# A cross-attention pair: VectorE transposes x of the first batch of every second pair from blocks

## The chip, the core and the metric

The kernel runs on one core of a Trainium2 chip. The metric is the device time of one execution in microseconds. The kernel before took 321.79, 327.54 and 326.51 us in three runs, median 326.51; the execution that was profiled took 321.73 us.

## The reference

Inputs are x and ctx (called y in the kernel), each 32 batches of 128 channels by 1024 positions, float32, and small weight matrices of 128 x 128. Two layers follow one another:

- Layer 0, twice a channel attention with 8 heads of 16 channels: queries from x, keys and values from y, and the other way round. The scores are sums over all 1024 positions, so each head has a 16 x 16 matrix; softmax over its rows; values times attention, and a projection. The two results are added to x + y.
- Layer 1: queries and keys from y (with biases), values from the output of layer 0, again channel attention with 8 heads, an output projection, a residual, and a normalisation over all 128 x 1024 elements of a batch with a gain and shift per channel.

```
attn = softmax(einsum('bhni,bhnj->bhij', q, k) * scale)      # layer 0, both directions
scores = einsum('bhdl,bhel->bhde', q, k) / sqrt(E)            # layer 1
o = Wo @ (attn @ v) + bo + x;  o_hat = (o - mean) * rsqrt(var + eps) * gn_w + gn_b
```

## The kernel before

Since all scores are sums over positions, the kernel never forms queries or keys. For each batch it computes one Gram matrix of (y, 1, x) over positions (gram_chunks), 128 x 257, and gets the scores of all three attentions from it with weight products (u12_products, u3_products, scores). The attention matrices are folded with the weights into one matrix per input (z_products, m_products, pq_products), P for x and Q for y, and the output is P x + Q y + shift (out_half), with each operand split into a high part and a low rest. pq_high (ScalarE) and pq_low (VectorE) split P and Q; split_high (ScalarE) and split_low (GpSimd) split x and y. Then come the moments and the normalisation.

Work goes in steps step(h, u), one for each pair of batches p = 2h + u; the four batches of an h are n = 4h + 2u + b with a buffer (slot) 2u + b each. A step does the Gram matrices of pair p, the scores and attention of pair p - 1, and the output of pair p - 2. Steps 2 to 15 take the branch `front` with `back` set; of these, u = 1 holds for h = 1 to 7. From h = 2 the steps lie in a hardware loop with two steps in a pass.

A Gram matrix needs positions on the partitions, so x and y must be transposed into the tile t (positions x (y, 1, x)). This is done in two ways. TensorE transposes x of the first batch of a pair (b = 0) from the natural layout (x_transpose of the PE block, L345), four 128 x 128 pieces a call into the PSUM tile tpx, and ScalarE copies each half into t (xt_out, L637). VectorE transposes y of both batches and x of the second from y_blocks and x_blocks (y_transpose L867, x_transpose L877), tiles that the DMA has already loaded with the blocks rearranged so that 32 x 32 transposes finish the job. A half batch is one such instruction.

Every engine runs its list in the written order, and semaphores order the engines: xt_ready and yt_ready (halves transposed), n_ready (n3_out on VectorE done, L1020), pq_done, pqhi_ready, pqlo_ready, u3_ready, attn_ready. Two PSUM banks called mid0 and mid1 are used in turn: u12_products, then the scores in mid0; pq_products, then u3_products in mid1. pq_low reads mid1 after pq_high has; so u3_products waits for pqlo_ready of its own step. u12_products waits for c_ready (c_out), and z_operands, before the last chunk of the pair's Gram matrices, for attn_ready.

The SP queue loads what comes next in its own order: for each step refill_blocks of the first batch, refill_raw of a batch of the pair before, refill_blocks of the second batch (with load_x_blocks), refill_raw of the first batch. Each waits until the buffer is free.

In the order of TensorE before the change, the front of each step is

```
x_transpose(h, u, 0)
pq_products(p - 2)
x_transpose(h, u, 1)
u12_products(p - 1)
out_half(h - 1, u, 0, 0)
u3_products(p - 1)
```

Of the kernel before, what the change touches and what calls it, by code (L numbers as in the profile page):

```python
# [6 lines left out]
B, C, N, H = 32, 128, 1024, 8  # L7
# [3 lines left out]
HC = CH // 2  # L11
HALF = N // 2
QUADS = 4
# [14 lines left out]
def cross_attention_pair_kernel(nc, x, y, weights, vectors, quad_rows, consts, out):  # L28
# [13 lines left out]
    with ctx:  # L42
        def sb(name, shape, dt=f32):
            return ctx.enter_context(nc.sbuf_tensor(name, shape, dt))
# [4 lines left out]
        def sem(name):  # L49
            return ctx.enter_context(nc.semaphore(name))  # L50
# [23 lines left out]
        mask6 = sb("mask6", [C, 6, W32])  # L74
        raw = [sb(f"raw{n}", [C, 2, N]) for n in range(4)]
        y_blocks = [sb(f"y_blocks{n}", [C, QUADS, N // QUADS]) for n in range(4)]
        x_blocks = [sb(f"x_blocks{n}", [C, QUADS, N // QUADS]) for n in range(2)]
        xy_hi = [sb(f"xy_hi{n}", [C, 2, N], f32r) for n in range(4)]
        xy_lo = [sb(f"xy_lo{n}", [C, 2, N], f32r) for n in range(4)]

# [54 lines left out]
        x_in = [sem(f"x_in{n}") for n in range(4)]  # L135
        y_in = [sem(f"y_in{n}") for n in range(4)]
        blocks_in = [sem(f"blocks_in{n}") for n in range(4)]
        x_blocks_in = [sem(f"x_blocks_in{n}") for n in range(2)]
        x_half_in = [sem(f"x_half_in{n}") for n in range(2)]
        y_half_in = [sem(f"y_half_in{n}") for n in range(2)]  # L140
        stored = [sem(f"stored{n}") for n in range(4)]
# [70 lines left out]
        def before(h, u):  # L212

            return (h - 1, 0) if u == 1 else (h - 2, 1)
# [7 lines left out]
        @block.sync  # L222
        def _(sp):
            def load_x(h, n):
                sp.dma_start(raw[n][:, 0, :], x[4 * h + n]).then_inc(x_in[n], 16)

            def load_y(h, n):
                sp.dma_start(raw[n][:, 1, :], y[4 * h + n]).then_inc(y_in[n], 16)

            def load_blocks(h, n):  # L230

                blocks = y[4 * h + n].rearrange("(i c) (a m) -> a c i m", c=W32, a=QUADS)
                for a in QUAD_ORDER:
                    sp.dma_start(y_blocks[n][W32 * a:W32 * (a + 1), :, :], blocks[a]).then_inc(blocks_in[n], 16)

            def load_x_blocks(h, u):

                blocks = x[4 * h + 2 * u + 1].rearrange("(i c) (a m) -> a c i m", c=W32, a=QUADS)
                for a in QUAD_ORDER:
                    sp.dma_start(x_blocks[u][W32 * a:W32 * (a + 1), :, :], blocks[a]).then_inc(x_blocks_in[u], 16)  # L240

            sp.dma_start(cst[:, :], consts).then_inc(consts_in, 16)
            for i in range(2):
                cols = slice(HALF * i, HALF * (i + 1))
                sp.dma_start(raw[0][:, 0, cols], x[0][:, cols]).then_inc(x_half_in[i], 16)
                sp.dma_start(raw[0][:, 1, cols], y[0][:, cols]).then_inc(y_half_in[i], 16)
            load_x(0, 1)
            load_y(0, 1)
            sp.dma_start(vec[:, :], vectors).then_inc(weights_in, 16)
            sp.dma_start(quad[:, :, :], quad_rows).then_inc(weights_in, 16)  # L250
            sp.dma_start(wt[:, :, :], weights).then_inc(weights_in, 16)
            k = WNAMES.index("prT")
            sp.dma_start(w_rot[0:H64, :, :], weights[H64:C, k:k + 2, :]).then_inc(weights_in, 16)
            sp.dma_start(w_rot[H64:C, :, :], weights[0:H64, k:k + 2, :]).then_inc(weights_in, 16)
            for n in range(2, 4):
                load_x(0, n)
                load_y(0, n)
            load_blocks(1, 0)
            load_blocks(1, 1)
            load_x_blocks(1, 0)  # L260

            def raw_free(h, u, b):

                n = 4 * h + 2 * u + b
                sp.wait_ge(split_hi, 2 * n + 2)
                sp.wait_ge(split_lo, 2 * n + 2)
                if isinstance(n, int) and n < 4:
                    sp.wait_ge(y_early_done, 2 * n + 2)
                    sp.wait_ge(x_transposed[b], n - b + 2)
                elif b == 0:  # L270
                    sp.wait_ge(x_transposed[0], n + 2)

            def refill_raw(h, u, b):
                raw_free(h, u, b)
                load_x(h + 1, 2 * u + b)
                load_y(h + 1, 2 * u + b)

            def refill_blocks(h, u, b):
                n = 4 * h + 2 * u + b
                sp.wait_ge(yt_ready, 2 * n + 2)  # L280
                load_blocks(h + 1, 2 * u + b)
                if b == 1:
                    sp.wait_ge(xt_ready[1], n + 1)
                    load_x_blocks(h + 1, u)

            def store(h, u, b):
                q = 4 * h + 2 * u + b - 4
                sp.wait_ge(normed, q + 3)
                if q == B - 1:
                    sp.wait_ge(last_normed, 1)  # L290
                sp.dma_start(out[q], res[2 * u + b][:, :]).then_inc(stored[2 * u + b], 16)

            def step(h, u):
                refill_blocks(h, u, 0)
                refill_raw(h - 1 + u, 1 - u, 1)
                refill_blocks(h, u, 1)
                refill_raw(h, u, 0)

            refill_raw(0, 0, 0)
            load_blocks(1, 2)  # L300
            refill_raw(0, 0, 1)
            load_blocks(1, 3)
            load_x_blocks(1, 1)
            refill_raw(0, 1, 0)
            with sp.Fori(1, PAIRS // 2 - 1) as i:
                step(i, 0)
                step(i, 1)
            last = PAIRS // 2 - 1
            refill_raw(last - 1, 1, 1)
            store(last + 1, 0, 0)  # L310
            store(last + 1, 0, 1)
            store(last + 1, 1, 0)
            store(last + 1, 1, 1)
            for n in range(4):
                sp.wait_ge(stored[n], 16 * (B // 4 + 1))
# [3 lines left out]
        def _(pe):  # L319
# [15 lines left out]
            def x_transpose(h, u, i):  # L335

                p = 2 * h + u
                if i == 0:
                    pe.wait_ge(x_in[2 * u], 16 * (h + 1))
                if isinstance(p, int) and p == 2:  # L340
                    pe.wait_ge(xt_ready[1], 3 + i)
                pe.wait_ge(xt_ready[0], 2 * p - 1 + i)
                chunks = raw[2 * u][:, 0, :].rearrange("c (r m) -> c m r", m=CH)
                for c in range(HC):
                    mm = pe.transpose(tpx[i][:, c, :], chunks[:, HC * i + c], ident)  # L345
                mm.then_inc(x_transposed[0], 1)
# [188 lines left out]
            def step(h, u, front, middle, back, post):  # L535
# [32 lines left out]
                    gram_full_width(h, u, 1, 5, 8)  # L568
                    m_products(p - 1, False)
                elif front:  # L570
                    x_transpose(h, u, 0)
                    pq_products(p - 2)
                    x_transpose(h, u, 1)
                    u12_products(p - 1)
                    out_half(h - 1, u, 0, 0)
                    u3_products(p - 1)
                    if post:
                        group_moments(p - 3)
                    out_half(h - 1, u, 0, 1)
# [49 lines left out]
        def _(act):  # L629
            def xt_out(h, u, b, i):  # L630

                slot = 2 * u + b
                n = 4 * h + slot
                act.wait_ge(x_transposed[b], 2 * (2 * h + u) + i + 1)
                if i == 0 and not (isinstance(n, int) and n < TB):
                    act.wait_ge(gram_done, n - TB + 1)
                act.activation(t[slot][:, HC * i:HC * (i + 1), XC:GW], tpx[i][:, :, :], ACT.Copy)\  # L637
                    .then_inc(xt_ready[b], 1)
# [95 lines left out]
            def step(h, u, front, middle, back, post):  # L734
# [23 lines left out]
                    z_out(p - 1)  # L758
                    gram_out(p, 1)
                elif front:  # L760
                    xt_out(h, u, 0, 0)
                    pq_high(p - 2, u)
                    xt_out(h, u, 0, 1)
                    u12_out(p - 1)
                    split_high(h - 1 + u, 1 - u, 1, 0, post)
                    keys_times_sums(p - 1)
# [49 lines left out]
        def _(dve):  # L816
# [49 lines left out]
                dst = t[slot][:, HC * i:HC * (i + 1), 0:C].rearrange("p m (i c) -> p m i c", c=W32)  # L866
                dve.transpose(dst, blocks[:, HC * i:HC * (i + 1)]).then_inc(yt_ready, 1)  # L867

            def x_transpose(h, u, i):

                n = 4 * h + 2 * u + 1
                if i == 0:
                    dve.wait_ge(x_blocks_in[u], 16 * QUADS * h)
                    dve.wait_ge(gram_done, n - TB + 1)
                blocks = x_blocks[u][:, :, :].rearrange("p i (c m) -> p m i c", c=W32)
                dst = t[2 * u + 1][:, HC * i:HC * (i + 1), XC:GW].rearrange("p m (i c) -> p m i c", c=W32)
                dve.transpose(dst, blocks[:, HC * i:HC * (i + 1)]).then_inc(xt_ready[1], 1)  # L877

            def gram_mirror(p):

# [148 lines left out]
            def step(h, u, front, middle, back, post, ahead=True):  # L1029
# [7 lines left out]
                elif front and not back:  # L1037
# [10 lines left out]
                    n3_out(p - 1)  # L1048
                    c_out(p - 1, 1 - u)
                    gram_mirror(p)  # L1050
                elif front:
                    if post:
                        half_stats(*before(h, u), 1, 1)
                        half_moments(p - 3)
# [4 lines left out]
                    u3_out(p - 1)  # L1059
                    if post:  # L1060
                        variance(p - 3, 1 - u)
                    x_transpose(h, u, 0)
                    shift_scores(p - 1)
                    x_transpose(h, u, 1)
                    softmax_out(p - 1)
                    half_stats(h - 1, u, 0, 0)
                    half_stats(h - 1, u, 0, 1)
                    if ahead:
                        y_transpose(h + u, 1 - u, 0, 0)
                        y_transpose(h + u, 1 - u, 0, 1)  # L1070
                    gram_mirror(p)
                    half_stats(h - 1, u, 1, 0)
                    n12_out(p - 1)
# [131 lines left out]
```

## Time and profile before

| | before |
|---|---|
| median of 3 runs | 326.51 us (321.79 to 327.54) |
| profiled execution | 321.73 us |
| its span | 319.9 us |
| TensorE matmul busy | 307.0 us, 96% |
| TensorE weight load busy | 269.3 us, 84% |
| VectorE busy | 262.2 us, 82% |
| ScalarE busy | 233.0 us, 73% |
| GpSimd busy | 190.0 us, 59% |
| DMA | 73.87 MB, mean 231 GB/s |
| mean granted TensorE clock | 0.994 |

The span is the time from the first to the last instruction of the profiled execution; the device time includes what lies around it. Busy times are unions of the instructions' spans; matmuls overlap, so their mean duration is longer than the step from one to the next. The chain of waits, followed back from the last instruction, gives pieces without overlap.

### The profile page before, as it was taken

To read this page: it belongs to the slowest core of one execution; us is meant where nothing else is said; L and a number is where in the kernel's file an instruction comes from. 1 tells how busy PE (TensorE), PEld (TensorE's weight loads), DVE (VectorE), ACT (ScalarE), POOL (GpSimd) and SP (SyncE) were. 2 spreads that over 40 slices of the span, in tenths; PEclk is the share of its full clock that TensorE was granted. 3 is DMA by queue.
4 is the path that set the end of the run, shared out by engine and by line. 5 is a ranking of instruction groups with operands and counts; after the bars stand their busy time and mean duration, and the time that the engine had idled before them with its cause. 6 is when DMAs were issued, how large, how long until landed. Compare 5 with 4: busy or idle time off the path is not lost.

```text
span 319.9 us, 12574 instructions
## 1 busy us (share of the span) xinstructions
PE 307.0 (96%) x4792; PEld 269.3 (84%) x4792; DVE 262.2 (82%) x707; ACT 233.0 (73%) x385; POOL 190.0 (59%) x277
## 2 busy tenths in 40 slices
PE   7999999999998999999999999999999999999980
PEld 4887898988888798888989888898988889898760
DVE  2495897889998688988888899988888898976883
ACT  3654656878778577887878787797878779786485
POOL 0866291767656376664647676464667656465620
PEclk9999999999999999999999999999999999999997
DMA  7999969499896949979696978969696976130036
GB/s 223 386 276 321 280 189 274 120 299 232 270 308 185 310 141 309 256 226 324 181 317 192 304 228 275 310 168 332 190 291 204 304 220 207 56 131 0 2 131 262
DMA packets 39060, 73.87 MB, mean 231 GB/s; under 512 B 4608, under 2 KB 26368, under 8 KB 39040
## 3 DMA queue, kind: packets, MB, share of 16 engines
q1 hardware_dynamic: 35008, 58.92, 64.1%
q10 hardware_dynamic: 4032, 14.68, 13.2%
q8 instruction: 13, 0.21, 0.3%
q14 instruction: 7, 0.06, 0.1%
HBM read 56.81 MB, written 16.78 MB: 230 GB/s over the span
## 4 chain that ended last, share of the span: by engine, by line
PE 92%; DVE 2%; issue 2%; DMA 2%; ACT 1%; SPq 1%; POOLq 0%; POOL 0%
PE oacc L428 10%; PE oacc L435 9%; PE oacc L429 8%; PE mid L531 5%; PE gacc L388 4%; PE mid L455 4%; PE mid L508 4%; PE stat L390 4%; PE tpx L345 4%; PE gacc L389 3%; PE stat L388 3%; PE gacc L390 3%; PE stat L389 3%; PE mid L517 2%; PE gacc L406 2%; PE mid L518 2%
## 5 line engine op out<-in xcount | busy, mean ns | idle before, releaser
L1136 POOL TENSOR_TENSOR xy_lo<-raw,xy_hi 128x256 fp32r<-128x256 f32 x256 | 179.4, 739 | 113.5 <-ACT xy_hi L705 113.5
L705 ACT ACTIVATE xy_hi<-raw 128x1024 fp32r<-128x1024 f32 x64 | 67.0, 1049 | 0.0
L867 DVE STREAM_TRANSPOSE t<-y_blocks 128x512 f32<-128x512 f32 x56 | 62.4, 1154 | 0.0
L712 ACT ACTIVATE res<-oacc 128x512 f32<-128x512 f32 x59 | 34.9, 593 | 27.9 <-PE oacc L435 27.6
L428 PE MATMUL oacc<-xy_hi,pq_hi 128*128 128x512 f32 x120 | 52.3, 436 | 0.1
L896 DVE BATCH_NORM_STATS2 hstat<-res 128x6 f32<-128x512 f32 x60 | 40.1, 687 | 14.0 <-ACT res L712 14.0
L429 PE MATMUL oacc<-xy_lo,pq_hi 128*128 128x512 f32 x120 | 47.3, 394 | 0.5 <-issue 0.5
L391 PE MATMUL gacc<-t 128*32 128x225 f32 x224 | 45.3, 354 | 0.0
L390 PE MATMUL gacc<-t 128*32 128x225 f32 x224 | 45.3, 354 | 0.0
L391 PE MATMUL stat<-t 128*32 128x225 f32 x224 | 44.9, 353 | 0.0
L390 PE MATMUL stat<-t 128*32 128x225 f32 x224 | 44.9, 353 | 0.0
L389 PE MATMUL gacc<-t 128*32 128x161 f32 x224 | 44.3, 300 | 0.0
L389 PE MATMUL stat<-t 128*32 128x161 f32 x224 | 43.9, 299 | 0.0
L388 PE MATMUL stat<-t 128*32 128x129 f32 x224 | 43.0, 272 | 0.8 <-issue 0.8
L388 PE MATMUL gacc<-t 128*32 128x129 f32 x224 | 42.9, 273 | 0.0
L726 ACT ACTIVATE res<-res,nbias,nscale 128x1024 f32<-128x1024 f32 x30 | 37.2, 1242 | 5.2 <-issue 4.3
L435 PE MATMUL oacc<-xy_hi,pq_lo 128*128 128x512 f32 x120 | 38.6, 404 | 0.0
L392 PE MATMUL gacc<-t 128*32 128x96 f32 x224 | 36.8, 246 | 0.0
L392 PE MATMUL stat<-t 128*32 128x96 f32 x224 | 36.8, 246 | 0.0
L877 DVE STREAM_TRANSPOSE t<-x_blocks 128x512 f32<-128x512 f32 x28 | 31.9, 1139 | 0.0
L393 PE MATMUL gacc<-t 128*32 128x64 f32 x224 | 30.8, 219 | 0.0
L393 PE MATMUL stat<-t 128*32 128x64 f32 x224 | 30.7, 219 | 0.0
(166 smaller groups left out, 906.1 us busy)
## 6 DMA issues: line engine op xcount, KB each, us to landing
raw<-in_x SPq DMA_DIRECT2D x31, 512.0 KB, 5.2
raw<-in_ctx SPq DMA_DIRECT2D x31, 512.0 KB, 6.4
y_blocks<-in_ctx SPq DMA_DIRECT2D x112, 128.0 KB, 6.5
out<-res ACTq DMA_DIRECT2D x28, 512.0 KB, 3.4
x_blocks<-in_x SPq DMA_DIRECT2D x56, 128.0 KB, 6.3
out<-res SPq DMA_DIRECT2D x4, 512.0 KB, 2.7
wt<-in_weights SPq DMA_DIRECT2D x1, 896.0 KB, 7.0
raw<-in_x SPq DMA_DIRECT2D x2, 256.0 KB, 3.5
```

What stands on the lines that cost most here:

```text
L388: pe.matmul(acc[0:W32, C:GW], wa, tb[:, c, C:GW], start=first, stop=False)
L389: pe.matmul(acc[3 * W32:C, 3 * W32:GW], wd, tb[:, c, 3 * W32:GW], start=first, stop=False)
L390: pe.matmul(acc[W32:H64, W32:GW], wb, tb[:, c, W32:GW], start=first, stop=final)
L391: pe.matmul(acc[H64:3 * W32, W32:GW], wc, tb[:, c, W32:GW], start=first, stop=final)
L392: pe.matmul(acc[0:W32, 0:3 * W32], wa, tb[:, c, 0:3 * W32], start=False, stop=final)
L393: mm = pe.matmul(acc[3 * W32:C, 0:H64], wd, tb[:, c, 0:H64], start=False, stop=final)
L428: pe.matmul(bank[:, :], whi, xy_hi[slot][:, s, cols], start=(s == 0), stop=False)
L429: pe.matmul(bank[:, :], whi, xy_lo[slot][:, s, cols], start=False, stop=False)
L435: mm = pe.matmul(bank[:, :], pq_lo[u][:, b, s, :], xy_hi[slot][:, s, cols], start=False, stop=(s == 1))
L705: act.activation(xy_hi[slot][:, s, :], raw[slot][:, s, :], ACT.Copy).then_inc(split_hi, 1)
L867: dve.transpose(dst, blocks[:, HC * i:HC * (i + 1)]).then_inc(yt_ready, 1)
L1136: piece = pool.tensor_tensor(xy_lo[slot][:, s, cols], raw[slot][:, s, cols], xy_hi[slot][:, s, cols].bitcast(f32), ALU.subtract)
```

## The change

VectorE now also transposes x of the first batch (b = 0) of the pairs with u = 1, from a third x_blocks tile, so slots 1, 2 and 3 have one. TensorE's x_transpose and ScalarE's xt_out remain for u = 0 only. In the u = 1 steps u3_products moves in front of the first output half. On VectorE, the first half of that transpose stands at the end of the u = 0 step, and the u = 1 step has an order of its own: pq_low directly behind half_stats, then the moments, the second half of the transpose, and y_transpose in two separate calls around u3_out and variance. The SP queue loads the third tile (four DMAs of 128 KB) in the u = 1 step behind refill_raw, after a wait on xt_ready[0], and once at the start.

```diff
-        x_blocks = [sb(f"x_blocks{n}", [C, QUADS, N // QUADS]) for n in range(2)]
+        x_blocks = {n: sb(f"x_blocks{n}", [C, QUADS, N // QUADS]) for n in (1, 2, 3)}
...
 # SP
-                elif b == 0:
-                    sp.wait_ge(x_transposed[0], n + 2)
+                elif b == 0 and u == 0:
+                    sp.wait_ge(x_transposed[0], 2 * h + 4)
...
             def step(h, u):
                 refill_blocks(h, u, 0)
                 refill_raw(h - 1 + u, 1 - u, 1)
+                if u == 1:
+                    sp.wait_ge(xt_ready[0], 4 * h + 4)
+                    load_x_blocks(h + 1, 2)
                 refill_blocks(h, u, 1)
                 refill_raw(h, u, 0)
...
             refill_raw(0, 0, 1)
+            load_x_blocks(1, 2)
             load_blocks(1, 3)
-            load_x_blocks(1, 1)
+            load_x_blocks(1, 3)
...
 # TensorE
                 elif front:
-                    x_transpose(h, u, 0)
+                    if u == 0:
+                        x_transpose(h, u, 0)
                     pq_products(p - 2)
-                    x_transpose(h, u, 1)
+                    if u == 0:
+                        x_transpose(h, u, 1)
                     u12_products(p - 1)
+                    if u == 1:
+                        u3_products(p - 1)
                     out_half(h - 1, u, 0, 0)
-                    u3_products(p - 1)
+                    if u == 0:
+                        u3_products(p - 1)
...
 # ScalarE
-                    xt_out(h, u, 0, 0)
+                    if u == 0:
+                        xt_out(h, u, 0, 0)
                     pq_high(p - 2, u)
-                    xt_out(h, u, 0, 1)
+                    if u == 0:
+                        xt_out(h, u, 0, 1)
...
 # VectorE: x_transpose takes a batch b
-            def x_transpose(h, u, i):
+            def x_transpose(h, u, b, i):
+                slot = 2 * u + b
+                n = 4 * h + slot
                 if i == 0:
-                    dve.wait_ge(x_blocks_in[u], 16 * QUADS * h)
+                    dve.wait_ge(x_blocks_in[slot], 16 * QUADS * h)
                     dve.wait_ge(gram_done, n - TB + 1)
...
+                dve.transpose(dst, blocks[:, HC * i:HC * (i + 1)]).then_inc(xt_ready[b], 1)
...
 # VectorE, u = 0: as before, and at its end
+                    c_out(p - 1, 1 - u)
+                    x_transpose(h, 1, 0, 0)
 # VectorE, u = 1
+                elif front:
+                    half_stats(*before(h, u), 1, 1)
+                    pq_low(p - 2, u)
+                    half_moments(p - 3)
+                    partition_moments(p - 3, 1 - u)
+                    x_transpose(h, u, 0, 1)
+                    y_transpose(h, u, 1, 0)
+                    u3_out(p - 1)
+                    variance(p - 3, 1 - u)
+                    y_transpose(h, u, 1, 1)
+                    x_transpose(h, u, 1, 0)
+                    shift_scores(p - 1)
+                    x_transpose(h, u, 1, 1)
                     softmax_out(p - 1)
                     half_stats(h - 1, u, 0, 0)
                     half_stats(h - 1, u, 0, 1)
```

## Rows read from the trace of the kernel before

**Rows 1.** The page: busy us, share of the span, instructions of each engine.

```profile
PE 307.0 (96%) x4792; PEld 269.3 (84%) x4792; DVE 262.2 (82%) x707; ACT 233.0 (73%) x385; POOL 190.0 (59%) x277
```

**Rows 2.** Busy by window, one whole step: PE, PEld, DVE, ACT, POOL, clock, DMA, GB/s.

```profile
163.30:181.70 18.40, 18.37 (x319) 16.45 (x318) 16.25 (x43) 14.44 (x24) 11.94 (x18) 1.00 0.86 253
```

**Rows 3.** The chain of waits at the head of pair 9's step: start us, us, what.

```profile
163.33 0.44 PE tpx L345 x4
163.77 0.89 PE mid L531 x8
164.66 0.44 PE tpx L345 x4
165.10 0.87 PE mid L455 x4
165.97 0.23 PE oacc L428
...
167.35 0.44 PE mid L464 x4
167.80 0.12 PE stat L442 x2
...
169.41 0.25 PE mid L475 x8
```

**Rows 4.** Groups of instructions, TensorE's transposes: count, busy us, mean ns, idle before.

```profile
L345 PE MATMUL tpx<-cst,raw 128*128 128x128 f32 x112 | 16.9, 274 | 0.0
```

**Rows 5.** Timelines, pairs 0 and 2: start us, us, engine, line, idle before it.

```profile
20.01 0.71 PE L464 MATMUL mid<-wt,gram 128*128 128x128 f32 x4
...
33.27 0.43 DVE L1020 TENSOR_TENSOR nmat<-mid,cst 128x256 f32<-128x256 f32 x1
33.75 1.16 PE L531 MATMUL mid<-nmat 128*128 128x128 f32 x8
34.95 0.60 ACT L684 ACTIVATE pq_hi<-mid 128x512 fp32r<-128x512 f32 x1 [0.62 <-PE mid L531]
35.58 0.69 DVE L889 TENSOR_TENSOR pq_lo<-mid,pq_hi 128x512 fp32r<-128x512 f32 x1 [0.73 <-ACT pq_hi L684]
```

**Rows 6.** Timeline of VectorE from the end of pair 8's step through pair 9's.

```profile
162.86 0.42 DVE L1020 TENSOR_TENSOR nmat<-mid,cst 128x256 f32<-128x256 f32 x1
163.20 0.21 DVE L1026 TENSOR_SCALAR cshift<-mid,vec 128x2 f32<-128x2 f32 x1
163.99 0.70 DVE L896 BATCH_NORM_STATS2 hstat<-res 128x6 f32<-128x512 f32 x1 [0.58 <-ACT res L712]
...
165.50 0.68 DVE L889 TENSOR_TENSOR pq_lo<-mid,pq_hi 128x512 fp32r<-128x512 f32 x1
166.10 2.22 DVE L867 STREAM_TRANSPOSE t<-y_blocks 128x512 f32<-128x512 f32 x2
168.25 0.56 DVE L970 SCALAR_TENSOR_TENSOR u<-wt,gram,mid 128x128 f32<-128x128 f32 x2
...
173.74 0.36 DVE L990 TENSOR_REDUCE ssum<-mid 128x6 f32<-128x192 f32 x1 [0.95 <-ACT mid L668]
...
174.66 0.56 DVE L1005 TENSOR_TENSOR attn<-mid,sinv 128x384 f32<-128x384 f32 x1
...
179.87 0.70 DVE L896 BATCH_NORM_STATS2 hstat<-res 128x6 f32<-128x512 f32 x1 [0.29 <-ACT res L712]
```

**Rows 7.** The chain of waits, first Gram chunk and the end of the last.

```profile
170.04 0.27 PE gacc L388
...
176.40 0.60 PE mid L508 x16
```

**Rows 8.** Timelines of GpSimd and of the SP queue in pair 9's step.

```profile
170.40 0.70 POOL L1143 TENSOR_TENSOR rstd<-var,cst 128x2 f32<-128x2 f32 x1
...
174.00 0.35 SPq L225 DMA_DIRECT2D raw<-in_x  x1
...
178.01 2.53 SPq L240 DMA_DIRECT2D x_blocks<-in_x  x4
```

**Rows 9.** Busy by window, a stretch with idle TensorE; and the longest transpose.

```profile
28.00:32.00 4.00, 3.76 (x37) 2.64 (x36) 0.70 (x1) 2.10 (x4) 2.78 (x4) 1.00 1.07 322
...
L867 DVE STREAM_TRANSPOSE t<-y_blocks x56: 1060/1144/1237, 26.6 to 277.4; 128x512 f32<-128x512 f32 x56
```

More of the change, by code:

```diff
@@ L137, in cross_attention_pair_kernel @@
         blocks_in = [sem(f"blocks_in{n}") for n in range(4)]
-        x_blocks_in = [sem(f"x_blocks_in{n}") for n in range(2)]
+        x_blocks_in = {n: sem(f"x_blocks_in{n}") for n in (1, 2, 3)}
         x_half_in = [sem(f"x_half_in{n}") for n in range(2)]
@@ L234, in load_blocks, with load_x_blocks @@
                     sp.dma_start(y_blocks[n][W32 * a:W32 * (a + 1), :, :], blocks[a]).then_inc(blocks_in[n], 16)
-            def load_x_blocks(h, u):
-                blocks = x[4 * h + 2 * u + 1].rearrange("(i c) (a m) -> a c i m", c=W32, a=QUADS)
+            def load_x_blocks(h, n):
+                blocks = x[4 * h + n].rearrange("(i c) (a m) -> a c i m", c=W32, a=QUADS)
                 for a in QUAD_ORDER:
-                    sp.dma_start(x_blocks[u][W32 * a:W32 * (a + 1), :, :], blocks[a]).then_inc(x_blocks_in[u], 16)
+                    sp.dma_start(x_blocks[n][W32 * a:W32 * (a + 1), :, :], blocks[a]).then_inc(x_blocks_in[n], 16)
             sp.dma_start(cst[:, :], consts).then_inc(consts_in, 16)
@@ L259, in _ @@
             load_blocks(1, 1)
-            load_x_blocks(1, 0)
+            load_x_blocks(1, 1)
             def raw_free(h, u, b):
@@ L283, in refill_blocks @@
                     sp.wait_ge(xt_ready[1], n + 1)
-                    load_x_blocks(h + 1, u)
+                    load_x_blocks(h + 1, 2 * u + 1)
             def store(h, u, b):
@@ L633, in xt_out @@
                 n = 4 * h + slot
-                act.wait_ge(x_transposed[b], 2 * (2 * h + u) + i + 1)
+                if isinstance(n, int) and n < 4:
+                    act.wait_ge(x_transposed[b], 2 * u + i + 1)
+                else:
+                    act.wait_ge(x_transposed[0], 2 * h + 3 + i)
                 if i == 0 and not (isinstance(n, int) and n < TB):
@@ L867, in y_transpose @@
                 dve.transpose(dst, blocks[:, HC * i:HC * (i + 1)]).then_inc(yt_ready, 1)
-            def x_transpose(h, u, i):
-                n = 4 * h + 2 * u + 1
+            def x_transpose(h, u, b, i):
+                slot = 2 * u + b
+                n = 4 * h + slot
                 if i == 0:
-                    dve.wait_ge(x_blocks_in[u], 16 * QUADS * h)
+                    dve.wait_ge(x_blocks_in[slot], 16 * QUADS * h)
                     dve.wait_ge(gram_done, n - TB + 1)
-                blocks = x_blocks[u][:, :, :].rearrange("p i (c m) -> p m i c", c=W32)
-                dst = t[2 * u + 1][:, HC * i:HC * (i + 1), XC:GW].rearrange("p m (i c) -> p m i c", c=W32)
-                dve.transpose(dst, blocks[:, HC * i:HC * (i + 1)]).then_inc(xt_ready[1], 1)
+                blocks = x_blocks[slot][:, :, :].rearrange("p i (c m) -> p m i c", c=W32)
+                dst = t[slot][:, HC * i:HC * (i + 1), XC:GW].rearrange("p m (i c) -> p m i c", c=W32)
+                dve.transpose(dst, blocks[:, HC * i:HC * (i + 1)]).then_inc(xt_ready[b], 1)
             def gram_mirror(p):
@@ L1050, in step @@
                     gram_mirror(p)
-                elif front:
+                elif front and u == 0:
                     if post:
@@ L1061, in step @@
                         variance(p - 3, 1 - u)
-                    x_transpose(h, u, 0)
+                    x_transpose(h, u, 1, 0)
                     shift_scores(p - 1)
-                    x_transpose(h, u, 1)
+                    x_transpose(h, u, 1, 1)
+                    softmax_out(p - 1)
+                    half_stats(h - 1, u, 0, 0)
+                    half_stats(h - 1, u, 0, 1)
+                    y_transpose(h, 1, 0, 0)
+                    y_transpose(h, 1, 0, 1)
+                    gram_mirror(p)
+                    half_stats(h - 1, u, 1, 0)
+                    n12_out(p - 1)
+                    n3_out(p - 1)
+                    c_out(p - 1, 1 - u)
[10 more added lines that the diff above has]
+                    y_transpose(h, u, 1, 1)
+                    x_transpose(h, u, 1, 0)
+                    shift_scores(p - 1)
+                    x_transpose(h, u, 1, 1)
                     softmax_out(p - 1)
@@ L1068, in step @@
                     if ahead:
-                        y_transpose(h + u, 1 - u, 0, 0)
-                        y_transpose(h + u, 1 - u, 0, 1)
+                        y_transpose(h + 1, 0, 0, 0)
+                        y_transpose(h + 1, 0, 0, 1)
                     gram_mirror(p)
```

## The prediction

> **What bounds the kernel now.** I read the busy table first, then one step in the steady part, then its chain of waits, then the timelines of the two engines that the change touches. The table puts TensorE at 96% of the span and VectorE at 82% [rows 1]. In one whole step of the later part, a u = 1 step (pair 9), TensorE is busy for 18.37 of 18.40 us at full clock, VectorE for 16.25 [rows 2]. The steady step is therefore the sum of TensorE's own work, and anything TensorE need not do is worth its full length, provided that nothing makes it wait in its place. The busy time alone does not settle the price, since matmuls overlap; the chain gives the step from one piece to the next, and I take all prices from it.
>
> In that chain the head of the step has no idle piece [rows 3]: first group of four transposes 0.44 us, pq_products 0.89, second group of transposes 0.44 (164.66 to 165.10), u12_products 0.87, first half of the output 1.38 (165.97 to 167.35), u3_products 0.44 (0.45 by the starts), group_moments and the second half 1.61 (167.80 to 169.41), then scores. From 163.33 to 169.41 that is 6.08 us.
>
> **What is removed.** The reordered branch is the one for u = 1, h = 1 to 7: 7 steps. Each loses 8 TensorE transposes, 2 x 0.44 = 0.88 us, 6.2 us in all. As a check, the 112 transposes of the whole run are busy for 16.9 us [rows 4], which gives 8.4 for 56 by the busy time; that counts overlapped tails, so 6.2 stands and 8.4 is the far end of the gain. Two ScalarE copies per step go too; ScalarE waits elsewhere in the step and they are worth nothing by themselves.
>
> **What the transposes were hiding, at pq_products.** It waits for n3_out on VectorE, which ends at 162.86 + 0.42 = 163.28 [rows 6]. Before, four transposes ran in front of it. Now it is first. Pair 2's step shows a start straight after that wait: n3_out ends at 33.27 + 0.43 = 33.70, the matmuls begin at 33.75 and take 1.16 us to the end instead of the 0.89 of a running stream [rows 5]. So: start at 163.33, end at 164.49 rather than 163.33 + 0.89 = 164.22. Cost 0.27 us.
>
> **The wait that appears, at u3_products.** It writes the bank mid1, and its wait on pqlo_ready is met only by this step's pq_low, which reads the same bank. Where it stood, behind the first output half, that was past. Now only u12_products stands between. The path is pq_products, pq_high on ScalarE, pq_low on VectorE, then u3_products. Pair 2 shows its length: the products end at 33.75 + 1.16 = 34.91, pq_high starts at 34.95, and pq_low ends at 35.58 + 0.69 = 36.27 [rows 5], 1.36 us. From 164.49 this gives 165.85, and with 0.05 more to wake TensorE, 165.90. u12_products ends at 164.49 + 0.87 = 165.36. A restarted u3_products takes 0.71 us (pair 0, [rows 5]), so it ends at 166.61 instead of 165.80. Cost 0.81 us.
>
> VectorE could be later than that: in front of pq_low stands now x_transpose(h, 1, 0, 0), moved to the end of the u = 0 step, and half_stats. c_out starts at 163.20 with 0.21; one transpose steps on 1.08 (2.15 for two, 166.10 to 168.25) and half_stats 0.65 to 0.70 [rows 6]. 163.35 + 1.08 + 0.68 = 165.11, against pq_high's end at 164.49 + 0.04 + 0.60 = 165.13. The transpose fits into the 0.58 us that VectorE waited before half_stats, plus what the pq path leaves; nothing is added, but the margin is nil.
>
> **The sum.** Per step -0.88 + 0.27 + 0.81 = +0.20 us; scores would start at 169.61. Seven steps: +1.4 us. As lower end I let both restarts cost nothing beyond the idle time between slots: 0.16 (163.33 against the free slot, which lies one overlapped tail of about 0.16 before the end at 163.33) and 0.70, so -0.02 per step, or -0.1 in all; 0.1 us of error in the hand-offs in the good direction makes it -0.8. Upper end: pq_low later by the 0.16 that a transpose of its longest kind here shows over its step (two of them, 2.22 with tails, against 2.15, and 0.1 for half_stats' wait on its input) and collisions below: +0.6 per step, +4. I take +1.4 since pair 2's rows are the same instructions in the same order.
>
> **The rest of the step, costed at nothing.** From pq_low's start to attn's end before: 165.50 to 174.66 + 0.56 = 175.22, 9.72 us, of which 0.95 was idle before the sum of exponents [rows 6]. VectorE now has in this stretch one more transpose (1.08) and the moments (0.8, from behind half_stats to 165.50), and no idle: pq_low starts at 165.16, so attn ends at 165.16 + 8.77 + 1.88 = 175.81. TensorE wants it before the last of 16 gram chunks, 170.04 to 176.40 at 0.40 each, so at 176.0 [rows 7], now 176.2. Slack 0.4 us. GpSimd's rstd started at 170.40 [rows 8], bound by its own subtractions, which start about 0.6 earlier as ScalarE skips two copies; variance comes about 0.4 later; these cancel. The step's tail on VectorE (next y, gram_mirror, half_stats) had 0.29 idle before the last half_stats and starts 0.6 late on a TensorE that is 0.2 late: tight, at most 0.1. The next u = 0 step keeps its order.
>
> The SP queue gains a wait on xt_ready[0] and four issues of 128 KB between raw and y_blocks. The wait is met at about 167.6 while SP only comes there at 174 or later, so nothing queues behind it. The y_blocks, x_blocks and raw loads behind it move by one group of issues, 2.5 us for four [rows 8]; their tiles are read a whole loop pass (36 us) after they come free, so this is hidden. Traffic in a pass rises from 18 to 19 half-megabyte transfers, so from this step's 253 GB/s [rows 2] to about 267. POOL's queue gets no new step.
>
> **A rule that speaks against.** TensorE kept its full clock (1.00, the 2.4 GHz level) in the stretch 28 to 32 us although 0.24 us of it was idle [rows 9]; the new idle is about 0.6 us in one piece per step, and I take no loss from it. The Trainium skill, "TensorE: Matmul & The Clock Gate", section "The HAM clock gate", says activity releases the throttle and idleness brings it back; no run here yet shows what gaps of this size do, and it is a rival below. By this rule the sum would lose in every such step.
>
> **Rivals.** (1) Faster: the stall at u3_products is not there or small, because pq_low comes sooner than pair 2's rows let it. For it: VectorE has spare time; against it: the path has three hand-offs, each seen in the trace, with one 0.87 us piece to cover 1.36. With no wait at u3_products: 7 x (-0.61) = -4.3, 322.2; with both waits gone -6.2, 320.3; only at the busy-time price, -8.4, 318.1, would it pass 2%.
> (2) Slower: attention arrives late. Place: z_operands, before the last gram chunk, on TensorE. It decides from 0.4 us of further delay on VectorE, then one for one. Four or five transposes in that stretch at 1.24 each (the longest seen, [rows 9]) instead of 1.08 would use 0.8: 0.4 beyond the slack, 7 x 0.4 = +2.8, with the rest +4.2, 330.7. To pass 2% it takes 0.7 us beyond. For it: VectorE has no idle left in this stretch.
> (3) Slower: the clock falls after the new idle. If the second half of the output (1.61) ran at the 1.2 GHz level in each step, +1.6 x 7 = +11, with the rest 339. Against it [rows 9].
>
> **Time, range and chances.** The profiled execution took 321.73 us (span 319.9), below the 326.51 median of the three runs (321.79 to 327.54). Against its own time the sum is 323.1; on the median, 327.9. The time of the changed kernel may show either level, so the range goes from 321.7 - 0.8, about 321, to 326.5 + 4, 330.5. Forecast (no measurable change, -0.8 to +4): 0.72. Rival 1: 0.12, of which 0.05 past 2% (the far price, or a median at the quick level). Rival 2: 0.12, 0.04 past 2%. Rival 3: 0.04, all past it. About 2% is what a measurement of this kernel tells from no change. So faster 0.05, same 0.87, slower 0.08.
>
> **What would show it.** Right: L345 with 56 matmuls; in u = 1 steps an idle of about 0.5 to 0.7 us before u3_products, released by pq_low, and pq_products restarting on n3_out; steps of u = 1 at about 18.5 to 18.6 us, u = 0 unchanged; attn ending less than 0.4 us before the last chunk. Wrong: u = 1 steps shorter than 18.2 (rival 1), an idle before the last chunk or z_products released by attn (rival 2), a granted clock under 1.00 in the steps (rival 3). The prediction fails most easily if a hand-off over three engines is shorter or longer than pair 2 shows, or if VectorE's fuller queue delays something I costed at nothing.

## The result, and the profile after

The changed kernel is slower by a little. Over 20 runs each its median is 324.66 us (322.51 to 329.3) and that of the kernel before 322.94 us (321.12 to 327.54); the ratio is 1.0061, 95% interval 1.0036 to 1.0085, so +2.0 us (+1.2 to +2.7 at 323 us). Single runs of one kernel spread by some 2%, so the ratio is taken over undisturbed runs alone. The profiled execution took 325.26 us, span 323.5.

The page of the changed kernel, busy us, share of the span and instructions of each engine, against [rows 1]:

```profile
PE 305.2 (94%) x4736; PEld 262.1 (81%) x4736; DVE 275.0 (85%) x721; ACT 228.9 (71%) x371; POOL 190.9 (59%) x277
```

56 matmuls fewer on TensorE, 14 transposes more on VectorE. TensorE has less to do, and the span is longer. Where the time went shows in the chain of waits at the head of pair 9's step, the counterpart of [rows 3] (start us, us, what):

```profile
165.15 0.57 PE oacc L439 x2
165.74 1.17 PE mid L535 x8
166.94 0.61 ACT pq_hi L696
167.56 0.70 DVE pq_lo L904
168.27 0.14 issue
168.40 0.68 PE mid L468 x4
169.09 0.23 PE oacc L432
...
170.47 0.12 PE stat L446 x2
170.59 0.34 PE oacc L432
...
172.08 0.25 PE mid L479 x8
```

Before, this chain had only TensorE in it. Now it leaves TensorE after pq_products (L535), goes over ScalarE's pq_high and VectorE's pq_low, and comes back at u3_products (L468). In the whole execution u3_products waits for pq_low seven times, once in each u = 1 step, 4.5 us in all. From the end of the previous output, 165.72, to scores, 172.08, are 6.36 us; it was 6.08. The weight loads of the same stretch (in brackets: the idle time before, and what ended it) show both stalls:

```profile
165.74 0.97 PEld L535 LDWEIGHTS mid<-nmat 128*128 128x128 f32 x8 [0.45 <-DVE nmat L1035]
166.63 0.73 PEld L459 LDWEIGHTS mid<-wt,gram 128*128 128x128 f32 x4
168.37 0.52 PEld L468 LDWEIGHTS mid<-wt,gram 128*128 128x128 f32 x4 [1.01 <-issue]
```

And the whole steps of pairs 9 (u = 1) and 10 (u = 0), columns as in [rows 2]:

```profile
165.72:184.36 18.64, 17.99 (x311) 15.75 (x311) 18.15 (x45) 13.85 (x22) 12.20 (x18) 1.00 0.87 257
184.36:202.72 18.36, 18.35 (x317) 16.06 (x316) 16.31 (x44) 14.47 (x24) 11.62 (x17) 1.00 1.01 284
```

In the u = 1 step TensorE is idle 0.65 us and VectorE is busy 18.15 of 18.64; the clock stays at 1.00, its 2.4 GHz level. The u = 0 step is as it was.

To compare kernels I use one number: the time from the first matmul of z_products in one step to that in the next, in the loop's later part, where it repeats within 0.08 us. It comes from the one profiled execution of each kernel, the ratio from all its runs.

```
kernel                                         u = 1 step   u = 0 step   ratio, 95% interval
before                                         18.36        18.36        1
changed                                        18.62        18.36        1.0061 (1.0036-1.0085)
before, u3_products early                      18.96        18.36        1.0134 (1.0071-1.0196)
changed, u3_products back                      18.46        18.36        1.0041 (1.0004-1.0078)
changed, u3_products in its own bank           18.49        18.36        1.0019 (0.9995-1.0044)
u3 back, x of first batch not transposed       18.13        18.35        0.9949 (0.9915-0.9984)
u3 back, u3_out first                          18.25        18.36        0.9999 (0.9960-1.0037)
u3 back, both x halves in the u = 0 step       18.11        18.36        0.9952 (0.9924-0.9980)
  and n_ready covered                          18.32        18.36        0.9963 (0.9927-0.9998)
  and n_ready covered, pqhi wait last          18.33        18.36        0.9978 (0.9949-1.0006)
  and pqhi wait last                           17.85        18.36        0.9925 (0.9895-0.9955)
own bank, both x halves in the u = 0 step      17.77        18.36        0.9870 (0.9818-0.9921)
```

Seven steps of +0.26 make +1.8 us, inside the measured +1.2 to +2.7. The profiled execution alone differs by 3.6 us in its span. About 2 us of that is one idle stretch of TensorE in pair 2's step, put down to issue (the profile shows nothing that the engine waited for), which no other step of this execution repeats:

```profile
46.11 1.87 issue
```

The kernel before had smaller ones at other places (0.81 us before L388, 0.46 before L429). Ten of the twelve profiles here hold one or two such stretches of 0.46 to 1.87 us, and a difference of two single profiles holds them too.

### The profile page after: what moved, and what is told of

It reads as the page before. It is cut to its first block, busy times and chain, and to the rows that moved or that the text cites. A ratio compares the mean times of both kernels' runs of the same rounds, so it can differ in the third digit from the quotient of the medians.

```text
span 323.5 us, 12537 instructions
## 1 busy us (share of the span) xinstructions
PE 305.2 (94%) x4736; PEld 262.1 (81%) x4736; DVE 275.0 (85%) x721; ACT 228.9 (71%) x371; POOL 190.9 (59%) x277
## 4 chain that ended last, share of the span: by engine, by line
PE 89%; DVE 3%; issue 2%; ACT 2%; DMA 2%; SPq 0%; POOLq 0%; POOL 0%
PE oacc L432 10%; PE oacc L439 9%; PE oacc L433 8%; PE mid L535 5%; PE gacc L392 4%; PE mid L512 4%; PE stat L394 4%; PE gacc L393 3%; PE gacc L394 3%; PE stat L393 3%; PE mid L468 3%; PE stat L392 3%; PE mid L521 2%; PE gacc L410 2%; PE mid L459 2%
## 5 line engine op out<-in xcount | busy, mean ns | idle before, releaser
L892 DVE STREAM_TRANSPOSE t<-x_blocks 128x512 f32<-128x512 f32 x42 | 47.9, 1141 | 0.0
L394 PE MATMUL stat<-t 128*32 128x225 f32 x224 | 45.4, 353 | 0.1
L395 PE MATMUL stat<-t 128*32 128x225 f32 x224 | 45.4, 353 | 0.0
L396 PE MATMUL stat<-t 128*32 128x96 f32 x224 | 36.9, 246 | 1.9 <-issue 1.9
L396 PE MATMUL gacc<-t 128*32 128x96 f32 x224 | 36.8, 246 | 0.0
```

The costliest lines, as they stand in the source:

```text
L394: pe.matmul(acc[W32:H64, W32:GW], wb, tb[:, c, W32:GW], start=first, stop=final)
L395: pe.matmul(acc[H64:3 * W32, W32:GW], wc, tb[:, c, W32:GW], start=first, stop=final)
L396: pe.matmul(acc[0:W32, 0:3 * W32], wa, tb[:, c, 0:3 * W32], start=False, stop=final)
```

## The experiments

The theory: what costs is the path n3_out, pq_products, pq_high, pq_low, u3_products, which the transposes and the first output half used to hide. The rivals: VectorE's added load costs by itself (18.15 us busy in the u = 1 step, 16.25 before; the 2.27 us in the expectation below is more than that difference); or the extra DMA does.

**u3_products put back.**

```diff
-                    if u == 1:
-                        u3_products(p - 1)
                     out_half(h - 1, u, 0, 0)
-                    if u == 0:
-                        u3_products(p - 1)
+                    u3_products(p - 1)
```

> The changed kernel with u3_products in the u = 1 steps put back behind the first output half, all else as changed. Theory (the hand-off stall): the wait for pq_low is then covered by the output half, and the 0.87 us that u12_products and u3_products took beyond their own 1.31 in pair 9 goes. The head of the step, from the end of the previous output to scores, falls from 6.36 to about 5.5 us. But VectorE does not move: in the changed kernel attn ended at 178.10, and TensorE would now want it at 178.65 - 0.87 = 177.78, so about 0.3 to 0.4 us comes back as a new wait before the last Gram chunk. u = 1 steps about 18.15 us (18.39 before, 18.62 changed), so about 1.7 us under the kernel before, ratio 0.995. Rival (VectorE's 2.27 us more per step is what costs): the position of u3_products does not matter, the step stays near 18.6 and the ratio at 1.006. Rival (no limit by VectorE at all): 17.75 us a step, ratio 0.986.

Measured: 18.46 us, ratio 1.0041. The stall before u3_products is gone, but of its 0.86 us only 0.16 came back, where 18.15 us a step and 0.995 were expected. The expectation was wrong in size, between theory and rival. The chain of waits shows why, and not at the place I had named (attention):

```profile
163.95 1.17 PE mid L535 x8
...
165.15 0.61 ACT pq_hi L693
...
166.91 0.04 DVE mom L932
...
167.25 1.08 DVE t L889
168.32 1.07 DVE t L878
169.40 0.50 DVE u L982 x2
169.90 0.14 issue
170.03 0.30 PE mid L479 x6
```

Behind pq_low VectorE does the moments, half of x (L889), half of y (L878) and only then u3_out (L982), and scores (L479) waits for it. In the changed kernel this line reads

```profile
171.12 0.61 DVE L985 SCALAR_TENSOR_TENSOR u<-wt,gram,mid 128x128 f32<-128x128 f32 x2
```

so u3_out ended at 171.73 and scores began at 172.08: a slack of 0.35 us that I had not looked up. A second loss: the first output matmul now follows u12_products directly and meets pq_high's end.

```profile
164.84 0.73 PEld L459 LDWEIGHTS mid<-wt,gram 128*128 128x128 f32 x4
166.08 0.19 PEld L432 LDWEIGHTS oacc<-xy_hi,pq_hi 128*128 128x128 f32 x1 [0.50 <-issue]
```

The kernel without the transposes, below, puts this second loss at 0.37 us and the first at 0.33, and 0.86 - 0.37 - 0.33 is the 0.16 that came back.

**The early u3_products alone, in the kernel before.**

```diff
                     u12_products(p - 1)
+                    if u == 1:
+                        u3_products(p - 1)
                     out_half(h - 1, u, 0, 0)
-                    u3_products(p - 1)
+                    if u == 0:
+                        u3_products(p - 1)
```

> The kernel before with one edit: in the u = 1 steps u3_products stands in front of the first output half; both groups of transposes stay on TensorE, VectorE's order is the old one. Theory (hand-off stall): pq_low ended at 166.18 in pair 9 and u12_products at 165.97, so with 0.05 to 0.14 to wake and 0.71 for the restarted products u3_products would end at 166.94 to 167.03 instead of 166.41, so 0.5 to 0.6 us more per step, 3.5 to 4.4 us in all, ratio 1.011 to 1.014, with nothing of the transposes changed. Rival (VectorE's load costs): nothing is added to VectorE, ratio 1.000.

Measured: 18.96 us, +0.60, ratio 1.0134, with no transpose moved and nothing added to VectorE. This is the theory's upper figure, and the rival's 1.000 lies outside the interval. The chain has the same ending:

```profile
166.92 0.69 DVE pq_lo L892
167.61 0.14 issue
167.75 0.68 PE mid L464 x4
```

**u3_products early, in a bank of its own.**

```diff
-            def u3_products(p, last=False):
+            def u3_products(p, last=False, own_bank=False):
-                if not last and not (isinstance(p, int) and p < 1):
+                if not (last or own_bank) and not (isinstance(p, int) and p < 1):
                     pe.wait_ge(pqlo_ready, p)
...
-                    mm = pe.matmul(u3_bank[last][...
+                    mm = pe.matmul(u3_bank[last or own_bank][...
```

> The changed kernel, u3_products still early in the u = 1 steps, but written to a PSUM bank that is free there (tpx0), so that it need not wait for pq_low's read of mid1; u3_out reads it there. Theory (the wait is for mid1 and pq_low): no idle before u3_products, the 0.87 us go as in the run with the old position, and VectorE's late attention takes 0.3 to 0.4 of it back: u = 1 steps 18.15 us, ratio 0.995. Rival (u3_products stalls for its operand, the mirrored Gram matrix, or for issue): the idle before it stays, ratio 1.006.

Measured: 18.49 us, ratio 1.0019. The idle before u3_products is gone, so it was the wait for mid1 and pq_low, not its operand or issue. The rest of the expectation (18.15 us, 0.995) was missed as in the first run, by the same u3_out: in the waits of the later part (us in total, times, longest) TensorE waits for it in 5 steps, 0.7 us at most, where u3_products put back had 0.3.

```profile
PE mid L479 <- DVE u L985: 3.4, 5, 0.7
```

TensorE came 0.4 us sooner and waited 0.4 longer: VectorE set the time of scores in both.

**Without VectorE's transposes of the first batch.**

```diff
+                if b == 0:
+                    dve.memset(gate[:, 0:1], 0.0).then_inc(xt_ready[0], 1)
+                else:
+                    dve.transpose(dst, blocks[:, HC * i:HC * (i + 1)]).then_inc(xt_ready[b], 1)
```

> As the kernel with u3_products put back, but VectorE's two transposes of the first batch's x in the u = 1 steps are left out (a one-element memset signals in their place; the DMA loads stay), so that part of x is never refreshed. Theory: VectorE is 2.2 us lighter per step, attn comes 1 to 2 us before the last Gram chunk, no wait there; u = 1 steps 17.75 us, the price of the transposes on TensorE less the 0.3 us that pq_products waits for n3_out; ratio 0.986. The difference to the run with the transposes is what VectorE's load costs once the stall is gone: 0.3 to 0.4 us per step. Rival (VectorE never limits): equal to that run. Rival (extra DMA costs): this run too stays slow, near 1.000.

This kernel leaves the two transposes out and serves only to time the rest. Measured: 18.13 us, ratio 0.9949 (0.9915 to 0.9984); 17.75 us and 0.986 were expected, and that was missed. The difference to the run with the transposes was met. So VectorE's load costs 18.46 - 18.13 = 0.33 us per step in that order, the size I had expected, but through scores. The extra DMA loads are in this kernel, and its step is what the chain adds up to: 18.36 - 0.88 + 0.30 (pq_products) + 0.37 = 18.15. Nothing is left for the DMA. The 0.37, which the expectation left out, is the first output matmul, 0.11 idle and 0.49 where [rows 3] has 0.23:

```profile
163.37 0.87 PE mid L459 x4
164.23 0.11 issue
164.34 0.49 PE oacc L432
```

**u3_out first.**

```diff
-                    y_transpose(h, u, 1, 0)
                     u3_out(p - 1)
+                    y_transpose(h, u, 1, 0)
```

> As the kernel with u3_products put back, and on VectorE u3_out moved in front of y_transpose(h, u, 1, 0) in the u = 1 steps. There the scores had waited for u3_out (pair 9: moments, x half, y half, u3_out to 169.90, scores at 170.03 where TensorE was free at about 169.6). Theory: this wait, 0.3 to 0.45 us per step, goes, and late attention takes little back (attn ended at 176.25, last Gram chunk wanted at 176.6 less 0.4): u = 1 steps from 18.46 to about 18.1 us, 2.5 us under that kernel, ratio about 0.996. Rival (VectorE's total work sets the step, whatever its order): the wait only moves to the last Gram chunk, the step stays near 18.4, ratio 1.002 to 1.004.

Measured: 18.25 us, ratio 0.9999. TensorE no longer waits for u3_out, and 0.21 of the expected 0.36 us came back. The ratio's interval (0.9960 to 1.0037) holds the theory's figure and the rival's; the steps and the waits tell more. What is missing against the kernel without the transposes, 0.12 us, stands at the last Gram chunk: attn ended at 174.57 + 0.56 = 175.13, and the chunk's first weight load began 0.05 us later.

```profile
174.57 0.56 DVE L1017 TENSOR_TENSOR attn<-mid,sinv 128x384 f32<-128x384 f32 x1
...
175.18 0.11 PEld L392 LDWEIGHTS stat<-t 128*32 128x32 f32 x1
```

This is the second rival of the prediction, seen at last, though it took two freed stalls to get there.

**Both halves of x in the u = 0 step.**

```diff
 # u = 0
                     x_transpose(h, u, 1, 1)
+                    x_transpose(h, 1, 0, 0)
                     softmax_out(p - 1)
...
                     c_out(p - 1, 1 - u)
-                    x_transpose(h, 1, 0, 0)
+                    x_transpose(h, 1, 0, 1)
 # u = 1
-                    x_transpose(h, u, 0, 1)
                     y_transpose(h, u, 1, 0)
```

> As the kernel with u3_products put back, and both halves of the first batch's x are transposed in the u = 0 step before: the first half where VectorE idled 0.84 us for the exponentials, the second where the first stood. The u = 1 steps get 1.07 us less on VectorE. Theory (VectorE's queue, not its total, costs): u3_out and attn both come 1.07 us earlier, neither wait is left, and u = 1 steps come down to the level of the kernel without those transposes, 18.13 us; u = 0 steps at 18.36 to 18.45. Ratio 0.995 to 0.997. Rival (total work on VectorE): the u = 0 steps grow by what the u = 1 steps lose, ratio near 1.003.

Measured: 18.11 and 18.36 us, ratio 0.9952, as expected; the rival's 1.003 lies outside the interval. The u = 1 step is that of the kernel without these transposes, and the u = 0 step has not grown. VectorE runs the same 721 instructions as in the kernel with u3_products back, so it was its queue in one stretch and not its total that cost.

**Covering the wait for n3_out, and the order of waits.** The first edit moves two output matmuls behind m_products and n12_out, n3_out, c_out ahead of half_stats in the u = 0 step, and pq_low ahead of half_stats in u = 1; the second moves one wait.

```diff
 # TensorE, u = 0
-                    out_half(h - 1, u, 1, 1, parts=(0,))
+                    out_half(h - 1, u, 1, 1, parts=(0,), ss=(0,))
                     m_products(p - 1, False)
+                    out_half(h - 1, u, 1, 1, parts=(0,), ss=(1,), bank_free=0)
...
 # second edit, in out_half
-                        if b == 0:
-                            pe.wait_ge(pqhi_ready, 2 * h + u + 1)
                         pe.wait_ge(split_hi, 2 * n + 2)
                         pe.wait_ge(split_lo, 2 * n + 2)
...
+                    if half == 0 and b == 0:
+                        pe.wait_ge(pqhi_ready, 2 * h + u + 1)
```

> As the previous kernel (both x halves in the u = 0 step), and at the end of the u = 0 steps two of the output's matmuls move behind m_products, and VectorE does n12_out, n3_out, c_out ahead of half_stats; in the u = 1 steps pq_low goes ahead of half_stats. Theory: pq_products need no longer wait for n3_out after the output's last matmul (0.30 us with the restart), which then starts about 0.4 us earlier than TensorE is free. u = 1 steps 17.8 to 17.9 us, another 2 us off, ratio about 0.989. Rival (the next thing behind is as late): half_stats, now later on VectorE, delays u3_out or attention and the step stays near 18.1.

> As the previous kernel, and in out_half the wait on pqhi_ready stands last of the four waits instead of first. In the kernel with u3_products put back, pq_high ended at 165.76 in pair 9 and the first weight load behind its wait started at 166.08, 0.32 us later, while single waits let TensorE go after 0.05 to 0.14. Theory (the waits behind the late one are worked off one by one): 0.1 to 0.2 us less per u = 1 step, 1 us in all, ratio 0.003 lower than the previous kernel; u = 0 steps, where pq_high is long done, unchanged. Rival (the 0.32 us is restart cost): no change.

Measured: 18.32 and 18.33 us, ratios 0.9963 and 0.9978. The first edit failed: 17.8 to 17.9 us were expected, and the step grew from 18.11. Its m_products were asked for 0.46 us sooner than before and met z_out, which ScalarE ends no sooner:

```profile
160.14 0.30 PEld L521 LDWEIGHTS mid<-z,wt 128*128 128x128 f32 x2 [0.52 <-ACT z L693]
162.49 1.09 PEld L535 LDWEIGHTS mid<-nmat 128*128 128x128 f32 x8
```

pq_products (L535) do run without idle now, so the restart was moved, not removed. The second edit, expected to give 0.1 to 0.2 us, changed no step. With it the idle before the first output fell from 0.50 to 0.22 us of weight-load time, but group_moments then waited 0.31 us for the moments, late because half_stats had gone behind pq_low:

```profile
165.33 0.19 PEld L432 LDWEIGHTS oacc<-xy_hi,pq_hi 128*128 128x128 f32 x1 [0.22 <-ACT pq_hi L698]
...
167.56 0.30 PEld L446 LDWEIGHTS stat<-mom,cst 128*128 128x128 f32 x2 [0.31 <-DVE mom L937]
```

So on this base the pair could not tell the order of waits from the restart.

**The order of waits alone, on the better base.** The second edit above, on the kernel with both halves of x in the u = 0 step.

> The kernel with both x halves in the u = 0 step (u = 1 steps 18.13 us), and in out_half the wait on pqhi_ready last of the four instead of first. There the first output matmul behind u12_products ends 0.60 us after it (0.11 idle and 0.49) where it took 0.23 in the kernel before, 0.37 us lost per step. Theory (single waits are worked off after the late one): 0.1 to 0.3 us back per u = 1 step, 17.85 to 18.0 us, ratio 0.990 to 0.993. Rival (restart cost only): 18.1 us, ratio 0.995.

Measured: 17.85 us against 18.11, ratio 0.9925 (0.9895 to 0.9955), as expected. The order of the waits was worth 0.26 of the 0.37 us. The ratios of the two kernels overlap in their intervals (0.9924 to 0.9980 there), so the 0.26 rests on the steps, five of each kernel, of which none of one comes near any of the other (17.84 to 17.90 against 18.10 to 18.17). pq_high ended at 167.35 + 0.60 = 167.95, and the first weight load behind it began 0.05 us later instead of 0.32:

```profile
168.00 0.19 PEld L432 LDWEIGHTS oacc<-xy_hi,pq_hi 128*128 128x128 f32 x1 [0.22 <-ACT pq_hi L693]
```

In the old order three waits that had been met stood behind the late one. In the kernel with u3_products back, for example, GpSimd's split of x and y had ended at 164.20, about 1.5 us before pq_high (165.76).

**The version that the runs point to.** Own bank, both halves of x in the u = 0 step, u3_out directly behind the moments; an addition of edits shown above.

> Both x halves in the u = 0 step, u3_products early in the u = 1 steps but in its own free bank (no wait for pq_low), u3_out on VectorE directly behind the moments. Theory: u3_products now covers pq_high's end, so the 0.37 us before the first output matmul go as well, and of the listed losses only the restart of pq_products (0.30) is left: u = 1 steps 18.39 - 0.88 + 0.30 = 17.81 us, u = 0 steps 18.36, so 4.1 us under the kernel before, ratio 0.987. Rival (VectorE is late again once TensorE is this fast): attn ends less than 0.3 us before the last Gram chunk and the step stays at 18.0 or more.

Measured: 17.77 us, ratio 0.9870 (0.9818 to 0.9921), 4.2 us under the kernel before; 17.81 and 0.987 were expected. The head of the step has one stall left, the restart of pq_products:

```profile
162.37 0.58 PE oacc L439 x2
162.95 0.01 issue
162.96 1.16 PE mid L535 x8
164.12 0.87 PE mid L459 x4
164.98 0.44 PE tpx L468 x4
165.43 0.23 PE oacc L432
```

attn ended at 173.71 + 0.56 = 174.27, about 0.7 us before the last chunk.

## Why the prediction was right and wrong

**Wrong in what it called the result.** The forecast was "no measurable change" with 0.87 on within 2%, and the last part took about 2% as what a measurement can tell. The ratio's interval is 0.25% to each side, and +2.0 us is outside it: the kernel is slower. The sum itself said +1.4 us, slower, and I did not let it name the direction. The step that failed is this last one: it took "about 2%" as what can be told from no change, for which the prediction shows no row, and so turned a sum of +0.20 us per step into "no measurable change". The runs showed +0.26 per step and a ratio that is told from 1 at 0.6%. The chances rested on the same 2%: 0.87 stood on "same" and only 0.08 on "slower", though the sum and most of the range were slower.

**Wrong in level.** 327.9 us was the median of three runs, 326.51, plus 1.4. The median of twenty was 322.94, the profiled 321.73 close to it; 323.1, the sum against the profile's own time, was 1.6 under the measured 324.66. That 324.66 lies inside the stated 321 to 330.5 says little, since 4.8 of these 9.5 us are the distance between two measured times of the same kernel.

**The sum, term by term.** Transposes: 56 went, 0.44 us a group stays the price ([rows 3]; the sums of the later kernels close with it). pq_products: +0.27 predicted; the previous output ends at 165.72 and pq_products at 166.91, so 1.19 instead of 0.89, +0.30. u3_products: +0.81 predicted; from 166.91 to 169.08, 2.17 where u12_products and u3_products took 0.87 + 0.44, +0.86. The three-engine path measured 1.35 (166.91 to 168.26) against 1.36; what was too small was the wake-up, 0.14 after pq_low instead of 0.05, of which a restarted u3_products of 0.68 instead of 0.71 took a part back. Head of the step: +0.28 against +0.20; whole step +0.26. Seven steps: +1.8 against +1.4. The two terms were 0.03 and 0.05 short, and pair 2's rows ([rows 5]) were the right source.

**Costed at nothing, rightly.** SP's wait and four more DMAs, the DMA traffic (the run without the transposes), the u = 0 step, VectorE's position before pq_low (it waited 0.15 us for pq_high), the clock (1.00 with 0.65 us of idle per step). By the Trainium skill, "TensorE: Matmul & The Clock Gate", section "The HAM clock gate", idleness brings the throttle back. Gaps of this size did not do so in any of the profiles, nor did the 1.87 us at 46.11 (granted clock 1.00 from 45 to 50 us). Attention's slack was 0.55 us, predicted 0.4: attn ended at 177.54 + 0.56 = 178.10, and the last Gram chunk began at 178.65.

```profile
177.54 0.56 DVE L1020 TENSOR_TENSOR attn<-mid,sinv 128x384 f32<-128x384 f32 x1
```

**Costed at nothing by oversight.** u3_out behind two more transposes, with scores waiting. In this kernel the stall at u3_products hid it, with 0.35 us to spare, so it did not change the time; it did decide what each repair was worth.

**The rivals.** Faster: refuted, the stall is there in every u = 1 step. Late attention: not in the changed kernel; its mechanism appears once the other two waits are gone. The clock: refuted.

**Where the expected gain went.** 0.88 us per step were taken off TensorE: 0.30 went to pq_products, 0.86 to u3_products. With the stalls moved away 0.59 of the 0.88 is real (18.36 to 17.77). That the loss at u3_products is caused by its position and by the shared bank is shown by the runs that put it early in the kernel before (+0.60) and in its own bank (stall gone). The 0.30 at pq_products is read from the traces alone: 1.16 to 1.17 us wherever they follow the wait for n3_out, 0.89 behind the transposes. The one run that tried to cover this wait moved the stall elsewhere, so what it would give back is not shown.

## What to carry to other kernels

Work on the bounding engine may be hiding the hand-offs around it: before it is taken away, add up the path over the other engines between its two neighbours and compare it with what is left as cover. When one stall is cleared, look up the slack of every later wait in the step, since a repair is worth no more than the smallest of them unless that wait comes sooner too. And a sum that has a sign is a forecast, however small; say the sign, and give it against the profile's own time.

## What the runs showed of the hardware that was not expected

- A semaphore wait that is met late holds up the waits written behind it. pq_high ended at 165.15 + 0.61 = 165.76 and TensorE's weight load, with three met waits behind, started at 166.08, 0.32 us later; where the late wait stood alone or last, TensorE started 0.05 to 0.14 us after it was met. Putting the late wait last gave 0.26 us per step (18.11 to 17.85).
- A first matmul after a stall costs TensorE more than the idle time: pq_products take 1.16 to 1.17 us to the end instead of 0.89, u3_products 0.68 to 0.71 instead of 0.44, wherever they follow a stall in these profiles.
- Idle stretches put down to issue, up to 1.9 us, fall on changing steps, but not evenly: in five of the twelve profiles (1.87, 1.15, 1.11, 0.78 and 1.87 us, all of kernels with the changed order) one stands in pair 2's step, before L396. One of the five belongs to the slowest of its kernel's ten runs (322.61 us, median 320.83), so they need not come in each execution. What they are was not tested.
